# Attention that transposes the scores before the exponential, with every fourth row in a tile and the distance matrix stored for contiguous reads

## The reference

```python
h = _layernorm(x) * (1 + ca) + sa
q, k, v = heads(h @ Wq + bq), heads(h @ Wk + bk), heads(h @ Wv + bv)      # [16, 16, 512, 16]
pos_emb = dist_emb[pos_l - pos_r + M - 1]                                   # [512, 512, 16]
rel_q = jnp.einsum('bhld,lrd->bhlr', q, pos_emb)
rel_k = jnp.einsum('bhrd,lrd->bhlr', k, pos_emb)
scores = (jnp.einsum('bhqd,bhkd->bhqk', q, k) + rel_q + rel_k) / 4
probs = softmax(scores)
ctx = jnp.einsum('bhqk,bhkd->bhqd', probs, v)
x = x + ga * layernorm(ctx @ Wo + bo + h)
h = _layernorm(x) * (1 + cb) + sb
x = x + gb * (sum over the two experts chosen of h @ we[e].T + be[e])
```

## Time and profile before

| | |
|---|---|
| Time, median of 3 runs (lowest to highest) | 3550.53 us (3544.78 to 3551.01) |
| The profiled execution's own time | 3545.81 us |
| Its span, first to last instruction | 3544.3 us |
| Busy PE, DVE, ACT, POOL | 2759.8, 2474.6, 1770.8, 703.2 us |
| Mean granted TensorE clock | 0.814 of full speed |
| HBM read, written | 465.93 MB, 340.05 MB |
| DMA packets, of them under 2 KB | 905515, 809536 |

### The profile page before, as it was taken

The page is one execution under the profiler, slowest core; times in us unless marked ns, Lnnn a source line. Parts: engine busy times, 40 slices in busy tenths (PEclk is TensorE's granted clock), DMA queues, the critical chain, the costliest instruction groups (busy, mean ns, idle before and its releaser), DMA issues. The chain is left out here.

```text
span 3544.3 us, 68683 instructions
## 1 busy us (share of the span) xinstructions
PE 2759.8 (78%) x18124; PEld 1931.5 (54%) x18124; DVE 2474.6 (70%) x6213; ACT 1770.8 (50%) x3509; POOL 703.2 (20%) x715
## 2 busy tenths in 40 slices
PE   4676588787787787748888877888888588888887
PEld 2343577777677777625555544555555344444443
DVE  5665477676777677648888877888888566666664
ACT  2343354444454444348888877888888411111111
POOL 2432000000000000012212211212221223333334
PEclk7888566666666666668999998999999789999999
DMA  3999799989989989799999999999999501111110
GB/s 112 221 224 213 162 311 348 294 337 291 331 302 333 299 333 321 309 261 271 268 272 278 267 257 268 268 272 274 270 272 275 180 32 63 62 62 62 62 62 20
DMA packets 905515, 807.89 MB, mean 228 GB/s; under 512 B 236808, under 2 KB 809536, under 8 KB 870832
## 3 DMA queue, kind: packets, MB, share of 16 engines
q1 hardware_dynamic: 840112, 640.95, 60.5%
q0 software_dynamic: 29440, 98.07, 13.0%
q10 hardware_dynamic: 35840, 67.12, 8.3%
HBM read 465.93 MB, written 340.05 MB: 227 GB/s over the span
## 5 line engine op out<-in xcount | busy, mean ns | idle before, releaser
L1059 ACT ACTIVATE t_e<-t_neg,t_low 128x512 f32<-128x512 f32 x1024 | 739.6, 736 | 232.2 <-DVE t_low L1001 228.9
L676 ACT ACTIVATE d_r<-d_pq 128x1024 f32<-128x1024 f32 x512 | 531.7, 1050 | 608.0 <-PE d_pq L633 604.6
L710 DVE TENSOR_TENSOR d_r<-d_pk,d_r 128x1024 f32<-128x1024 f32 x512 | 616.1, 1223 | 272.9 <-ACT d_r L676 134.0
L1001 DVE CUSTOM_DVE_ANT_0 t_neg<-t_ps,t_r 128x512 f32<-128x512 f32 x1024 | 671.3, 687 | 24.3 <-issue 24.3
L644 PE MATMUL d_pk<-d_win,d_k 96*128 96x128 bf16 x4096 | 513.8, 295 | 216.0 <-DVE d_r L710 181.0
L927 PE MATMUL t_pt<-t_ident,t_e 128*128 128x128 f32 x4096 | 639.4, 279 | 1.4 <-DVE t_eT L1009 0.9
L917 PE MATMUL t_ps<-t_kb,t_qa 96*128 (+1 forms) x1024 | 402.0, 393 | 251.6 <-DVE t_low L1001 202.2
L644 PEld LDWEIGHTS d_pk<-d_win,d_k 96*128 96x128 bf16 x4096 | 445.6, 183 | 248.5 <-DVE d_r L710 213.6
L927 PEld LDWEIGHTS t_pt<-t_ident,t_e 128*128 128x128 f32 x4096 | 513.7, 144 | 110.4 <-ACT t_eT L1066 16.7
L633 PE MATMUL d_pq<-d_win,d_q 96*128 96x128 bf16 x4096 | 498.2, 287 | 62.9 <-DVE d_q L693 45.2
L633 PEld LDWEIGHTS d_pq<-d_win,d_q 96*128 96x128 bf16 x4096 | 442.4, 187 | 80.2 <-DVE d_q L693 45.8
(11 more groups left out here) (134 smaller groups left out, 2509.1 us busy)
## 6 DMA issues: line engine op xcount, KB each, us to landing
r_scratch<-d_r SPq DMA_DIRECT2D x256, 1024.0 KB, 14.2
t_r<-r_scratch SPq DMA_DIRECT2D x1024, 256.0 KB, 5.3
d_q<-q_chunks_scratch ACTq DMA_DIRECT2D x64, 512.0 KB, 10.8
d_q<-q_chunks_scratch ACTq DMA_DIRECT2D x128, 256.0 KB, 14.1
t_kb<-k_chunks_scratch POOLq DMA_DIRECT2D x32, 512.0 KB, 19.9
q_chunks_scratch<-a_part SPq DMA_DIRECT2D x96, 128.0 KB, 3.6
q_rows_scratch<-a_part SPq DMA_DIRECT2D x96, 128.0 KB, 2.2
k_chunks_scratch<-a_part SPq DMA_DIRECT2D x96, 128.0 KB, 3.5
```

The source lines that it names most:

```text
L676: nc.scalar.activation(r[lc % 2][:, n * QL:(n + 1) * QL, :], pq[n % 2][:], ACT.Copy).then_inc(q_out, 1)
L710: nc.vector.tensor_tensor(part, pk[n % 2][:].rearrange("p r l -> p l r"), part, ALU.add).then_inc(k_added, 1)
L1001: nc.vector.tensor_tensor_reduce(out=neg[:, L, :], in0=p_s[bank(j, L)][:], in1=r[:, j % RR, L].rearrange("p c r -> p (c r)"), scale=-0.25, ...
L1059: nc.scalar.activation(e[:, j % 2, L, :], neg[:, L, :], ACT.Exp, bias=low[:, j % 2, L:L + 1], scale=-1.0, accum_out=total[:, j // GH, L, j ...
```

## The change

**Layout.** `r_d[g]` becomes `[column tile][head][row][column]`: for one head and one column tile the 512 rows lie behind each other, 256 KB in a run. `attention` reads it as 128 partitions of 2 KB: partition p gets rows 4p to 4p + 3. So tile t now holds rows 4p + t ("every fourth row"), and the weights of `score` are read with a step of 4 elements. The context comes out in the order (t, p), and `experts` reads x and h and writes its result in the same order: 4 KB per partition in a run. The stores in `distances` still write 8 KB per head, at a new pitch (266240 bytes where it was 69632).

**Order of the work.** The transposes take `t_neg` itself instead of its exponential. POOL (tiles 0, 1) and ACT (tiles 2, 3) first subtract the row minimum in place; PE transposes; ACT then takes the exponential of two tiles at once from PSUM, 128 x 1024, straight into `t_eT`. The two kinds of copies of `t_pt` and the accumulated row sums are gone: v is extended by 16 columns of ones (`t_vx`, which POOL fills), so that `weigh` gives the row sums too; ACT copies `t_pc` to `t_cs`, PE turns the sums with four small matmuls (`sums`), DVE inverts, POOL widens, PE transposes (`widen`), DVE scales. `t_ps` has two banks instead of three and scores run one tile ahead; `t_pt` is two pairs of banks.

**Queues.** POOL issues no DMA in `attention` any more. SP issues all: r (four DMAs of 256 KB per head, after all four tiles of the head four before have been read), v, the stores of the context, and the seven loads of the next batch's q and k, behind the r loads of head 4 of each batch (`load_next`).

```diff
-RPITCH = TB * TB + 1024
+RPITCH = NT * TB * TB + 1024
...
-                                to = r_d[g][tile % NT, tile // NT, :, p * part * TB:(p + 1) * part * TB]
+                                to = r_d[g][tile // NT, :, bass.ds(tile % NT * TB * TB + p * part * TB, part * TB)]
...
-        p_s = [ps(f"t_ps{i}", [P, S]) for i in range(BANKS)]
-        p_t = [ps(f"t_pt{i}", [P, TT, P]) for i in range(BANKS)]
+        p_s = [ps(f"t_ps{i}", [P, S]) for i in range(2)]
+        p_t = [ps(f"t_pt{i}", [P, 2, TT, P]) for i in range(2)]
...
+                def subtract(n, j, t):
+
+                    pool.wait_ge(added, TT * n + t + 1)
+                    nc.gpsimd.tensor_scalar(neg[:, j % RING, t, :], neg[:, j % RING, t, :],
+                                            low[:, j % RING, t:t + 1], None, ALU.subtract).then_inc(pool_sub, 1)
...
+                def load_r(g, n, j):
+
+                    later(sp, added, TT * (n - RR + 1))
+                    for c in range(NT):
+                        src = r_d[g][c, n - g * P, 0:NT * TB * TB].rearrange("(p x) -> p x", x=TT * TB)
+                        sp.dma_start(r[:, j % RR, c].rearrange("p t r -> p (t r)"), src).then_inc(r_loaded[j % RR], 16)
...
+                def batch(g, pair, u):
+                    b = 2 * pair + u
+                    fixed = isinstance(b, int)
+                    for j in range(H):
+                        load_r(g, H * b + j, j)
+                        k = j // GH
+                        if j % GH == 0:
+                            load_v(b, k)
+                        if j % GH == 1 and (not fixed or BG * b + k >= 3):
+                            store(b + (k - 3) // BG, (k - 3) % BG)
+                        if j == 4 and (not fixed or 1 <= b < nb - 1):
+                            nxt = pair + u
+                            load_next((b + 1) // GB if fixed else g, nxt, 1 - u)
...
+                def score(n, j, t):
+
+                    later(pe, added, TT * n + t - 1)
+                    lhs = qa[:, 0, n % SLOTS, :].rearrange("r (p t) -> r t p", t=TT)[:, t, :]
+                    nc.tensor.matmul(p_s[t % 2][:], lhs, kb[:, :, n % SLOTS, :],
+                                     start=True, stop=True).then_inc(scored, 1)
+
+                def turn(n, j, t):
+
+                    if t < 2:
+                        pe.wait_ge(pool_sub, 2 * n + t + 1)
+                    else:
+                        pe.wait_ge(act_sub, 2 * n + t - 1)
+                    if t % 2 == 0:
+                        later(pe, exped, 2 * n + t // 2 - 1)
+                    for c in range(TT):
+                        last = nc.tensor.transpose(p_t[t // 2][:, t % 2, c, :],
+                                                   neg[:, j % RING, t, c * P:(c + 1) * P], ident[:])
+                    last.then_inc(turned, 1)
...
+                def exp(n, j, half, G):
+
+                    act.wait_ge(turned, TT * n + 2 * half + 2)
...
+                    to = eT[:, j // GH % 2, j % GH, :, 2 * half:2 * half + 2, :].rearrange("p c t q -> p t c q")
+                    nc.scalar.activation(to, p_t[half][:], ACT.Exp, scale=(1.0 if half else -1.0)).then_inc(exped, 1)
...
-        x_v = ins["x"].rearrange("b (t p) e -> b p t e", p=P)
-        h_v = h_d.rearrange("b (t p) e -> b p t e", p=P)
-        out_v = out.rearrange("b (t p) e -> b p t e", p=P)
+        x_v = ins["x"].rearrange("b (p t) e -> b p t e", t=TT)
+        h_v = h_d.rearrange("b (p t) e -> b p t e", t=TT)
+        out_v = out.rearrange("b (p t) e -> b p t e", t=TT)
```

More of the change, by code:

```diff
@@ new lines, in head @@
+                def head(step, j):
+                    n = U * step + j
+                    fixed = isinstance(n, int)
+                    if not fixed or n < NH:
+                        for t in range(2):
+                            subtract(n, j, t)
+                    if j % GH == 0 and (not fixed or 2 * GH <= n):
+                        widen(2 * step + j // GH - 2)
+                    if j % GH == 1 and (not fixed or n < NH):
+                        copy_v(step, j // GH)
+                for n in range(NH + GH + 1):
+                    head(n // U, n % U)
@@ new lines, in _ @@
+                for b in range(2):
+                    load(b)
+                for g in range(NG):
+                    first, last = g * GB // 2, (g + 1) * GB // 2 - 1
+                    for u in range(2):
+                        batch(g, first, u)
+                    with sp.Fori(first + 1, last) as pair:
+                        for u in range(2):
+                            batch(g, pair, u)
+                    for u in range(2):
+                        batch(g, last, u)
+                for k in range(BG - 3, BG):
+                    store(nb - 1, k)
@@ L909, in _ @@
+                for par in range(2):
+                    sp.wait_ge(ctx_stored[par], STORE * NGR // 2)
             @block.tensor
             def _(pe):
-                pe.wait_ge(ident_done, 1)
-                pe.wait_ge(pc_zero, 1)
-                def score(n, j, L, slot):
-                    later(pe, added, TT * n + L - since(j, L) + 1)
-                    nc.tensor.matmul(p_s[bank(j, L)][:], qa[:, 0, slot, L * P:(L + 1) * P], kb[:, :, slot, :],
-                                     start=True, stop=True).then_inc(scored, 1)
@@ L953, in head, with widen @@
+                def widen(G):
+                    pe.wait_ge(widened, G + 1)
+                    for t in range(TT):
+                        last = nc.tensor.transpose(p_i[:, t * P:(t + 1) * P],
+                                                   wide[:, t * GH:(t + 1) * GH, :].rearrange("p j w -> p (j w)"), ident[:])
+                    last.then_inc(spread, 1)
                 def head(step, j):
@@ L1040, in _ @@
-                for step in range(2):
-                    for j in range(U):
-                        head(step, j)
-                with dve.Fori(2, NH // U) as step:
-                    for j in range(U):
-                        head(step, j)
-                for j in range(GH + 2):
-                    head(NH // U, j)
+                            add(n, j, t, step)
+                        G = 2 * step + k // GT - 2
+                        if k % GT == 1 and (not fixed or 0 <= G < NGR):
+                            invert(G)
```

329 lines of the change are left out of this document (145 added, 184 removed).

## The result

The changed kernel takes 3603.93 us (median of 4 runs, 3599.76 to 3607.38); beside it the kernel before took 3547.66 (3543.21 to 3551.01, 4 runs). The ratio is 1.0159, with a 95% interval of 1.0141 to 1.0177: slower by 1.6%, 56 us. The prediction said 3541, range 3450 to 3620, with faster a little likelier than slower. The range holds the time, the sign of the forecast is wrong. The profiled execution of the change has a span of 3605.7 us.

The account below looks back on a forecast made before the run. Bound before: three full engines and, in turn, a never-full ring of r; afterwards PE alone. Stalls -31, pace +18, start and end +4 make -9 us: 3537 against the profiled execution, 3541 as median, range 3450 to 3620.

Parts of the forecast that it names:

- the sign of the forecast: Whole kernel: likeliest 9 us less than before; faster 0.46, same 0.11 with a little more, slower 0.43.
- The views and PE as the bound: Profile readings of `attention`; after the change PE alone sets the pace there, 3.98 us per head, with stalls once per batch.
- Pace, +18: Clean stretches of `attention`: PE needs 15.9 us per group, 3.98 per head against 3.91, over 256 heads.
- Batch loads, -31: Stalls in `attention` at loads of the next q and k: 14 loads cost 185 us against 215.9.
- The blocked time: SP's queue at a batch load, until r of head 5 lands: 25.9 us, with the load itself taken as 18.
- The reading behind it: `attention` before the change: held in turn by three full engines and a never-full ring of r, DMA engines lacking time.
- Weights with a step, 0: Weight loads of `score` at a step of 8 bytes: 98 ns as when packed, hidden behind the transposes.
- Start +2: Start of `attention`: the first r follows two batch loads, where part of it ran beside them; 2 us more.
- End +2: End of `attention`: sums, inverse, widening and scaling hang on the last `weigh`; 2 us more.
- A fast load on SP's queue: Rival: batch loads take 7.5 us on SP's queue and all 216 us of waits go, 3338 us; chance 0.13.
- A longer slot by two banks and strided weights: Rival: strided weight load enters PE's score-add loop, 0.07 us more per slot, 4.26 per head, 3597 us; chance 0.18.
- 2 KB reads no faster: Rival: r reads stay at 3.5 us a head and the ring refills slowly, +12 to +70, near 3580; chance 0.09.

Follow-up runs that it names:

- b_none: Kernel before without the 14 loads of the next batch's q and k in the loop and PE's waits for them (its floor): 3328.39 us, ratio 0.9376.
- e_none: Changed kernel without the 14 loads of the next batch's q and k in the loop and PE's waits for them (its floor): 3392.9 us, ratio 0.9561.
- e_unroll: Changed kernel with PE's loop over eight heads written out, without branch or wait against a register: 3577.65 us, ratio 1.0085.
- e_old: Kernel before with only r's new layout and reads, strided weights and the last stage's order; old arithmetic, three banks and old queues: 3535.81 us, ratio 0.9946.
- e_packed: Changed kernel with the weights of each score read packed, not with a step of 4: 3595.82 us, ratio 1.0127.
- e_poolq: Changed kernel with all batch loads issued from POOL's queue, at the same place in the order of heads: 3604.78 us, ratio 1.0153.
- e_inv: Changed kernel with DVE's inverse of the sums one tile later: 3602.31 us, ratio 1.0151.
- e_spread_late: Changed kernel with the seven loads spread over heads 4 to 10 and PE waiting right before the first score that reads the batch: 3522.51 us, ratio 0.9915.
- e_divide: Changed kernel with the sums spread by one full matmul and DVE's inverse taken of 128x512: 3783.69 us, ratio 1.0665.

## Why the prediction was wrong

**The views and PE as the bound: right.** PE alone is full in clean stretches and DVE is at 0.69; the DMA engines are at 0.82, well under 1.0; nothing outside `attention` moved; stalls stayed, 14 of them. POOL's share, said to be under three quarters, is 0.81, since a subtraction takes 1.56 and not the 1.04 I chose; the upper bound of 1.55 was the value. PE's 20.00 of 20 makes it likely that this cost nothing; it wasn't tried apart.

**Pace, +18: the step that failed.** Measured are the 64.5 us between the floors of b_none and e_none; from the first `scale` to the last it is 973.9 us in b_none and 1041.8 in e_none, 68 more. The clean pace is 4.22 and not 3.98 us per head, 0.97 us per group more than my 15.9. By PE's rows it goes: `sums` 0.82 instead of 4 x 0.15 (+0.22; I took it near the pace of a transpose, and each is two instructions with a full weight load); `weigh` 1.10 instead of 1.07, four times, and one long slot (+0.2); and the end of PE's loop, 1.1 us per two groups (+0.55), which the working didn't have at all. The last is shown by e_unroll; the two others are read from the trace. Before the change a loop end cost less: two groups took 31.27 us, and the one of them in which no loop ends 15.55 in its trace, so 0.2 for the end. I read PE's 29.90 of 30 as full, but at 15.3 us of work in 15.6 PE had some room for such losses. When I made it the only bound at 15.9, every loss on it had to be counted. That the range holds the measured time is owed to its width and not to its working.

**Batch loads, -31: right in kind, too large.** Measured -10: 15.8 against 15.1 us a load. The blocked time was put at 25.9 us, so 10.0 of idle time each, and half clock at 3.2. DVE's idle time is 175.0 / 14 = 12.5. In the stall shown PE's clock was 0.69 over 2080 to 2085, so it was back near 2083, 6 us after PE had started: 3, as forecast. The term that was short is the load: it landed 19.3 us after issue and not 18 as the median of the stage, and 22.3 in the stall shown. The 291 GB/s of 2070 to 2077 are its tail, 156 to 209 GB/s until 2073, and then r behind it at 396 (2074 to 2077), no less than the 381 I took. Idle time and clock add up to 15.5 against a net cost of 15.1. This term is 21 us of the 65 by which the forecast is off, the pace nearly all the rest.

**The reading behind it: wrong in one place.** I wrote that the ring of r was never full before the change, for want of DMA time. But r took 3.5 us a head against a pace of 3.91, so there was time to fill it. The traces agree: before the change DVE mostly ran dry 10.6 us after a batch load was issued, in e_old 12.5 us after, so the faster packets made the ring deeper by 1.9 us, half a head. e_old is faster by 0.5%, 19 us, where the share of the DMA engines fell by a fifth; how much more there would be without PE's wait for t_kb stays open. The rate itself was right.

**Weights with a step, 0:** 8 us by e_packed, 16 ns a load; of the bounds 98 and 178 it was near the one taken. The Trainium skill ("SBUF — State Buffer", the note on cachelines), by which it is free, is off by those 16 ns. **Start +2:** DVE's fifth add came at 1569.5 and not at 1561.1, so +8. **End +2:** from the end of the last `weigh` to the first DMA of the next stage it is 8.1 us (2852.4 to 2860.5) where it was 11.5 (2787.5 to 2799.0), so -3: the longer chain behind `weigh` is there, 4 us to `scale`, but from `scale` on it takes 4 us with the stores on SP's queue and took 11.5 with them on POOL's.

**The rivals.** A fast load on SP's queue: no, it took 19.3 us there, where it had taken 19.9 on POOL's, and e_poolq shows that in this kernel the queue is of no account. (Its sum has an error: with the 4.7 us of the median, 3545.8 - 216 - 21 + 18 + 2 comes to 3334, not 3338.) A longer slot by two banks and strided weights: its size (3597, 4.26 us per head) was near by luck, its mechanism was not there. e_packed and e_inv leave little of it; the long slots belong to the loop. It was right in one thing, that little room was left beside PE's slots. 2 KB reads no faster: no, 389 GB/s in e_spread_late when the ring refilled, and 391 in the change (2077 to 2080).

## What to carry to other kernels

When a change leaves one engine as the only bound, sum everything that this engine does in a loop step, the loop's end too: a loss that was nearly hidden while three engines were full now counts whole, here 26 us for a loop end every eight heads. A stall behind a prefetch of fixed depth was here about as long as the foreign transfer, with what lands behind it, less the depth. Another queue didn't change that. Spreading the transfer did, for 81 us, once the consumer's wait stood where the data is needed; with the old arithmetic it did not help (3566 against 3536 us). Before easing a resource, ask whether it was ever late in the stretch between stalls.

## What the runs showed of the hardware

- The loads of 16 to 48 partitions take DMA time out of proportion to their bytes: 127 to 160 GB/s with the engines at 0.97 to 1.05 (2060 to 2070 with the change), against 383 to 391 at 1.06 for r over 128 partitions (2077 to 2085). The Trainium skill ("SBUF — State Buffer", Door 1: the DMA port swizzle) has 16 neighbouring partitions on 4 of 16 ports, and 32 or the first 48 on 8. By that rule and the 389 GB/s of the refill a batch takes, as an estimate, 0.79 MB / 97 + 2.36 MB / 195 = 20 us, and the trace agrees with 19.3.
- The end of a loop step on a full PE cost 0.9 to 1.1 us (e_unroll), spread over several slots (1.07, 0.92 and 0.87 where 0.66 is the undisturbed one), and not only where the branch stands. The Trainium skill ("Advanced Engine Details and Errata", Control Flow Timing) puts a compare and branch at 108 ns; the measurement decides. Of the rest, 0.28 us are the two waits for the batch (e_none, 33.48 against 33.76 for two groups); what the remainder is was not tried.
- A POOL subtraction of a [128, 1] operand from 128x512 took 1.56 us, a POOL copy to 128x512 0.61 where the multiplication of before took 1.04. DVE's inverse takes 3.35 us for 512 columns (e_divide) and 0.26 for 16.
